# A fused attention and routed feed-forward kernel: x's second half rounded two beats later, and the first batch's ranks counted one tile a slot

## The reference, cut to what matters

```python
x = layernorm(x + attention(x))     # x: 8 x 1024 x 512, 16 heads of 32, causal, fp32
x = layernorm(x + ffn(x))
# ffn, for each of the 8 batches of 1024 tokens:
scores = einsum('bsd,d->bs', x, w_router)
top_scores, top_idx = top_k(scores, 512)
h = gelu(x[top_idx] @ W1 + b1)      # 512 -> 2048
x[top_idx] += sigmoid(top_scores)[:, None] * (h @ W2 + b2)
```

## Time and profile before

| | |
|---|---|
| median of 3 runs | 2547.9 us (2544.73 to 2549.32) |
| profiled execution | 2547.39 us, span 2545.7 us |
| mean granted clock of PE | 0.986 of full |
| attention, by the stretches of the trace | up to about 1797 us |
| feed-forward | the rest, PE busy throughout |

### The profile page before, as it was taken

How to read it: one execution, slowest core, us unless ns; L and a number is a source line. 1 busy time by engine, 2 the same in 40 slices (tenths; PEclk the granted TensorE clock), 3 DMA queues, 4 the chain that set the end, 5 groups by cost and what they waited for, 6 DMA issues and landing times.

```text
span 2545.7 us, 40833 instructions
## 1 busy us (share of the span) xinstructions
PE 2463.0 (97%) x14168; PEld 1824.9 (72%) x14168; DVE 1663.5 (65%) x4230; ACT 1190.7 (47%) x2035; POOL 1565.3 (61%) x1642
## 2 busy tenths in 40 slices
PE   8999999999999999999999999997999999999998
PEld 6666676766777677667767767763688888888886
DVE  7767677677776777767777777676555544553533
ACT  3665566566566556556656566555431111111110
POOL 2878778788887788778788877786232113121311
PEclk9999999999999999999999999998999999999999
DMA  4233435335344433434434344343420001010000
GB/s 174 89 126 127 146 138 191 126 125 177 127 149 159 144 134 135 171 128 169 141 127 159 129 165 149 136 159 96 158 84 28 31 26 42 25 34 25 24 27 17
DMA packets 167502, 287.45 MB, mean 113 GB/s; under 512 B 23241, under 2 KB 58121, under 8 KB 166026
## 3 DMA queue, kind: packets, MB, share of 16 engines
q1 hardware_dynamic: 160130, 267.99, 30.0%
q0 software_dynamic: 7168, 16.85, 2.1%
HBM read 116.97 MB, written 65.11 MB: 72 GB/s over the span
## 4 chain that ended last, share of the span: by engine, by line
PE 73%; POOL 7%; ACT 4%; issue 3%; DVE 2%; DMA 1%; SPq 0%; POOLq 0%; DVEq 0%; ACTq 0%
PE PS L1525 14%; PE PS L1504 13%; PE PS L1363 8%; PE PS L1451 8%; PE PS L1417 7%; PE PS L1469 7%; PE PS L1377 6%; PE PS L1371 6%; POOL Pa L830 5%; DMA h_s<-hs 1%; PE PS L1386 1%; ACT Pm L958 1%; POOL lnrs L843 1%; ACT hs L1011 1%; ACT xb L1013 1%
## 5 line engine op out<-in xcount | busy, mean ns | idle before, releaser
L830 POOL TENSOR_TENSOR Pa<-Pa,Pm 128x512 f32<-128x512 f32 (+1 forms) x602 | 740.7, 1255 | 108.2 <-ACT Pm L958 94.8
L1451 PE MATMUL PS<-Qp,Kp 128*128 128x512 f32 (+3 forms) x1536 | 490.9, 356 | 35.6 <-ACT Pm L958 20.1
L1417 PE MATMUL PS<-Kp,Qp 128*128 128x512 f32 (+3 forms) x1536 | 490.1, 354 | 13.7 <-DVE nm L1055 7.5
L958 ACT ACTIVATE Pm<-PS 128x512 f32<-128x512 f32 (+1 forms) x643 | 358.2, 568 | 278.6 <-PE PS L1451 240.1
L1055 DVE TENSOR_REDUCE nm<-PS 128x1 f32<-128x512 f32 x512 | 345.7, 688 | 181.8 <-PE PS L1417 181.4
L830 POOL TENSOR_TENSOR Pa<-Pa,P 128x512 f32<-128x512 f32 (+1 forms) x297 | 368.2, 1264 | 55.7 <-ACT P L958 49.2
L1451 PEld LDWEIGHTS PS<-Qp,Kp 128*128 128x128 f32 x1536 | 279.6, 191 | 115.4 <-ACT Pm L958 33.8
L1417 PEld LDWEIGHTS PS<-Kp,Qp 128*128 128x128 f32 x1536 | 281.0, 192 | 112.9 <-issue 43.5
L920 ACT ACTIVATE G<-PS,b1c 128x512 f32<-128x512 f32 x128 | 88.1, 688 | 539.7 <-PE PS L1504 539.7
L1063 DVE CUSTOM_DVE_ANT_0 PS<-PS,maskA 128x384 f32<-128x384 f32 (+3 forms) x512 | 245.7, 509 | 140.4 <-PE PS L1417 139.4
L1063 DVE CUSTOM_DVE_ANT_0 PS<-PS,maskA,nm 128x384 f32<-128x384 f32 (+3 forms) x512 | 266.3, 555 | 88.4 <-PE PS L1417 83.4
(11 more groups left out here) (143 smaller groups left out, 4237.4 us busy)
## 6 DMA issues: line engine op xcount, KB each, us to landing
Qp<-nat SPq DMA_DIRECT2D x192, 256.0 KB, 2.5
Kp<-nat SPq DMA_DIRECT2D x192, 256.0 KB, 2.9
o_s<-Of SPq DMA_DIRECT2D x64, 256.0 KB, 2.1
Ot<-o_s SPq DMA_DIRECT2D x64, 256.0 KB, 3.0
xb<-in_x SPq DMA_DIRECT2D x64, 256.0 KB, 3.0
h_s<-hs SPq DMA_DIRECT2D x64, 256.0 KB, 2.4
out<-xb SPq DMA_DIRECT2D x64, 256.0 KB, 2.5
x_raw<-in_xt SPq DMA_DIRECT2D x15, 1024.0 KB, 6.0
```

The lines of the kernel that those rows point to most:

```text
L830: e.tensor_tensor(to, to, probs(u, k)[:, h0:h0 + many, 0:w], ALU.add).then_inc(s["padd"], many)
L958: e.activation(probs(u, k)[:, hh[0]:hh[-1] + 1, 0:w], tile_bank(j)[:, 0:len(hh) * w].rearrange("p (h n) -> p h n", n=w), ACT.Exp).then_inc ...
L1417: ins = e.matmul(to, Qp[:, u % 4, h_, qt * P:qt * P + P], Kp[:, (2 * i + k0 // 512) % 4, h_, 0:w], start=True, stop=True)
L1451: ins = e.matmul(tile_bank(j)[:, x_ * w:x_ * w + w], Kp[:, (2 * i + k // 4) % 4, h_, k % 4 * P:k % 4 * P + P], Qp[:, u % 4, h_, 512 - w:51 ...
```

## The change

1. ACT makes the high parts of the second half of x (batches 1 to 7) at the 7th and 8th beat after its load, instead of the 5th and 6th; DVE its four low parts at beats 8 to 11 after the load, instead of 6 to 9 (so at 128b - 13 to 128b - 10). For the first half DVE's four low parts are spread over beats 6, 8, 10 and 12 after the load instead of 6 to 9.
2. Batch 0's ranks: count t stands 11 beats after output tile 32 + t (beats 697, 713, ..., 809, one a slot, in slots 43 to 50), the list at beat 825, POOL's eight scatters at beats 830, 842, ..., 914, the load of the list at 1024, the gather at 1026. The scratch of the comparison is the hs buffer of output tile 32 + t, already stored and scored by then; ACT waits for the count before it writes that buffer again.
3. The copy of the scores (`srow0`) gets 4 KB of its own, taken from `nat`, which keeps two buffers instead of three.
4. From beat 992 POOL's part of the LayerNorm stands ahead of the additions of its beat.
5. `w1_hi` is at beats 1022, 1024, 1026, 1028, 1038, 1040, 1042, 1044, and `w1_lo` two beats later.

```diff
+GATHER = 63 * 16 + 18
+NORM_FIRST = 62 * 16
...
-            srow0 = ff.enter_context(nc.sbuf_tensor("srow0", [P, N], F32))
-            cmpb0 = ff.enter_context(nc.sbuf_tensor("cmpb0", [P, N], BF16))
...
-        nat = sb("nat", [P, 3, 2, 512], F32R)
+        nat = sb("nat", [P, 2, 2, 512], F32R)
+        srow0 = sb("srow0", [P, N], F32)
...
-            return s["nat", T.nat[job] % 3], 48 * (T.nat[job] // 3 + 1)
+            return s["nat", T.nat[job] % 2], 48 * (T.nat[job] // 2 + 1)
...
+        x_hi, x_lo = {}, {}
+        for n, (b, c) in load_x.items():
+            first = 7 if b and c else 5
+            for half in range(2):
+                x_hi[n + first + half] = b, c, half
+            for k in range(KT):
+                x_lo[n + first + 1 + (2 * k if b and not c else k)] = b, c, k
...
-        rank_at = BEATS * (U - 1) - 2
-        rank_beat = {rank_at + 2 * t: t for t in range(TT + 1)}
-        list_beat = {rank_at + 2 * TT + 1 + t: t for t in range(TT)}
-        list_load, gather_beat = rank_at + 3 * TT + 2, rank_at + 3 * TT + 4
+        RANK_O = 8 * (B - 4)
+        rank_beat = {T.beat[T.o_jobs[RANK_O + t]] + 11: t for t in range(TT + 1)}
+        rank_at = min(rank_beat)
+        list_beat = {max(rank_beat) + 5 + 12 * t: t for t in range(TT)}
+        list_load, gather_beat = GATHER - 2, GATHER
...
-        w1_hi = {BEATS * (U - 1) + 14 + 2 * k: divmod(k, 2) for k in range(8)}
-        w1_lo = {BEATS * (U - 1) + 16 + 2 * k: divmod(k, 2) for k in range(8)}
+        w1_at = [BEATS * (U - 1) + x_ for x_ in (14, 16, 18, 20, 30, 32, 34, 36)]
+        w1_hi = {n: divmod(k, 2) for k, n in enumerate(w1_at)}
+        w1_lo = {n + 2: divmod(k, 2) for k, n in enumerate(w1_at)}
...
             for n in range(T.first, T.last):
+                norms = [o_number(j) for j in o_beat.get(n - 1, ())]
+                if n >= NORM_FIRST:
+                    for o in norms:
+                        layer_norm(o)
                 for u, k in T.steps_formed(n):
...
-                for j in o_beat.get(n - 1, ()):
-                    o = o_number(j)
...
+                if n < NORM_FIRST:
+                    for o in norms:
+                        layer_norm(o)
...
-                        if j >= 3:
-                            e.wait_ge(s["nat", j % 3], 48 * (j // 3))
-                        e.activation(nat[:, j % 3, 0, :], bank(job), ACT.Identity, bias=bA[:, col:col + 1]).then_inc(s["kq_hi"], 1)
+                        if j >= 2:
+                            e.wait_ge(s["nat", j % 2], 48 * (j // 2))
+                        e.activation(nat[:, j % 2, 0, :], bank(job), ACT.Identity, bias=bA[:, col:col + 1]).then_inc(s["kq_hi"], 1)
...
+                    if RANK_O + 2 <= o < RANK_O + TT + 2:
+                        e.wait_ge(s["v_rank"], 2 * (o - RANK_O - 1))
                     e.activation(hs[:, k, :], xb[:, k, :], ACT.Identity, bias=lnb[:, k, 0:1],
...
-                if n - 5 in load_x:
-                    split_x(*load_x[n - 5], 0)
-                if n - 6 in load_x:
-                    split_x(*load_x[n - 6], 1)
+                if n in x_hi:
+                    split_x(*x_hi[n])
...
-                        count_ranks(e, s, cs, sc[:, 0, :], srow0, cmpb0, t)
+                        e.wait_ge(s["score"], RANK_O + t + 1)
+                        count_ranks(e, s, cs, sc[:, 0, :], srow0, hs[:, (RANK_O + t) % 2, :].bitcast(BF16), t)
...
-                for k in range(KT):
-                    if n - 6 - k in load_x:
-                        split_x(*load_x[n - 6 - k], k)
+                if n in x_lo:
+                    split_x(*x_lo[n])
```

More of the change, by code:

```diff
@@ L691, in sync @@
                         dst = Kp[:, (2 * i + c) % 4, :, :]
-                    j = T.nat[job] % 3
+                    j = T.nat[job] % 2
                     for r, part in ((1, 0), (2, 1), (3, 0)) if job[0] == "Q" else ((1, 0), (2, 0), (3, 1)):
@@ L727, in sync @@
                 if n == rank_at - 2:
-                    for j in range(3):
-                        e.wait_ge(s["nat", j], 48 * (len(T.nat) // 3))
                     e.wait_ge(s["scd"], 16)
@@ L741, in sync @@
                 if n == list_load:
+                    for j in range(2):
+                        e.wait_ge(s["nat", j], 48 * (len(T.nat) // 2))
                     load_list(0)
@@ L779, in gpsimd @@
             e.memset(ones[:, :].bitcast(F32), 1.0).then_inc(s["ones"], 1)
-            links = 0
+            links = [0]
             def gather(b):
@@ L808, in keep, with layer_norm @@
                                 pattern=[[0, HG], [1, P]], channel_multiplier=-1).then_inc(s["keep"], 1)
+            def layer_norm(o):
+                k = o % 2
+                e.wait_ge(s["lmva"], o + 1)
+                if o >= 2:
+                    e.wait_ge(s["oset"], o - 1)
+                v = lmv[:, k, 1:2]
+                e.tensor_scalar(lrs[:, k, 0:1], v, EPS, 1.0, ALU.add, ALU.mult)
+                e.tensor_scalar(lrs[:, k, 1:2], v, 1.0 + EPS / 4, EPS * EPS / 4, ALU.mult,
+                                ALU.add).then_inc(s["p_link"], 1)
+                e.wait_ge(s["p_link"], links[0] + 1)
+                e.tensor_tensor(lrs[:, k, :], lrs[:, k, :], cs["half"][:], ALU.pow).then_inc(s["p_link"], 1)
+                links[0] += 2
+                e.wait_ge(s["p_link"], links[0])
+                e.tensor_scalar(lnb[:, k, :], lrs[:, k, :], lmv[:, k, 0:1], -1.0, ALU.mult,
+                                ALU.mult).then_inc(s["rs"], 1)
             for n in range(T.first, T.last):
+                norms = [o_number(j) for j in o_beat.get(n - 1, ())]
+                if n >= NORM_FIRST:
+                    for o in norms:
+                        layer_norm(o)
                 for u, k in T.steps_formed(n):
@@ L852, in gpsimd @@
                     e.tensor_scalar(w, w, 1.0, 2.0, ALU.add, ALU.mult).then_inc(s["p_link"], 1)
-                    e.wait_ge(s["p_link"], links + 1)
+                    e.wait_ge(s["p_link"], links[0] + 1)
                     e.tensor_tensor(w, w, cs["minus"][:], ALU.pow).then_inc(s["sig"], 1)
-                    links += 1
+                    links[0] += 1
                 if n in list_beat:
@@ L1098, in evacuate @@
                     e.wait_ge(s["kq_hi"], j + 1)
[L1099 to L1102, removed]
+                    if j >= 2:
+                        e.wait_ge(s["nat", j % 2], 48 * (j // 2))
+                    e.scalar_tensor_tensor(out=nat[:, j % 2, 1, :], in0=src, scalar=bA[:, col:col + 1],
+                                           in1=nat[:, j % 2, 0, :].bitcast(F32), op0=ALU.add,
                                            op1=ALU.subtract).then_inc(s["ev_v"], 1)
@@ L1585 @@
               "ghi", "glo", "dn", "q_clear", "k_ones")
-SLOTTED = {"xraw": 2, "of_st": 2, "nat": 3, "ost": 2, "hst": 2, "xb": 2, "lst": 2, "x0": 4, "rw": 8, "li": 2, "hg": 2, "fo": 4, "no_shift": 4}
+SLOTTED = {"xraw": 2, "of_st": 2, "nat": 2, "ost": 2, "hst": 2, "xb": 2, "lst": 2, "x0": 4, "rw": 8, "li": 2, "hg": 2, "fo": 4, "no_shift": 4}
 def program(nc, x, xt, wqkv, wo, bat, b_out, w_router, W1, b1, W2, b2, out):
```

## The result

The changed kernel takes 2579.15 us by the median of four runs (2568.61 to 2582.38), the kernel before 2546.32 us on the same chip (four runs, 2543.61 to 2549.32). The ratio is 1.0121, 95% interval 1.0102 to 1.014: slower, as forecast, by 31 us instead of 10 (33 by the medians), and 2 us beyond the upper end of the range. The profiled execution is the shortest of the four, 2568.6 us with a span of 2566.9; the other three have a mean granted clock of 0.983 or 0.984 instead of its 0.988.

The account below looks back on a forecast made before the run. PE, busy 97% of the span, was taken as the bound, so only its waits or half-clock time could be won. 2547.4 + 18 - 12.5 + 4 = 2556.9, say 2557 us; range, 8 in 10, 2532 to 2577.

Parts of the forecast that it names:

- part 1: Moving x's high and low parts at seven batch boundaries: +18 us, bounds -3 and +43.
- I take 1.0, nearer the median: Length assumed for each DVE low part before the second Q; median 0.69 us, at most 1.81, 1.64 beside POOL's additions.
- rival A': Each low part beside a POOL addition takes 1.64 us: fourth ready at 16.7, +30 us for x's beats, 2569 us; chance 0.14.
- The clock: PE's clock falls behind the new wait at the second Q: 1.7 us charged per batch, as behind the old 2.88 us wait.
- The exp: PE's 2.88 us wait for an exp where a batch begins: about 1.8 go, 1.0 us stays.
- The two short waits among the next exps: ACT's two x roundings, now among the next exps, cost PE perhaps 0.9 us; second Q reached about 11.9 us after K.
- The first half's spread: Spreading the first half's low parts costs 0.3 us a batch, 2 us in all (bounds 0 and 0.7 each).
- `nat`: Two buffers make the second Q's evacuation wait for K's copies: covered, 0; 0.5 us waits would give 2573, chance 0.05.
- Part 2: Last slots of the attention, freed of ranks, scatters and four W1 roundings: -12.5 us, bounds -4 and -19.
- First stretch: 1712 to 1747 us: rank counts leave DVE, POOL (27.1 of 35 us) then ends last; 6 us won, at most 7.9.
- Second stretch: 1747 to 1798 us: scatters leave POOL, W1 roundings leave ACT's exps; 6.5 us won with the clock, of 0 to 11.3.
- Part 3: Ranks in their new place, eight counts on DVE and eight scatters on POOL: +4 us, bounds 0 and 12.

## Why the prediction was right and wrong

Right in direction and in mechanism: the wait moved from the exp to the second Q at seven boundaries and weighs more than the end wins. Too low by 22 us: 16 of them in part 1 (18, measured 34 with x's beats alone), 6 in parts 2 and 3 (-8.5, measured -2 without x's beats).

**Part 1, the step that failed: "I take 1.0, nearer the median", and with it the score at its best 0.7.** The fourth low part was put at 9.2 + 1.1 + 0.7 + 0.8 + 3.0 = 14.8 us after the K. Measured, in the same order: low part 2 begins at 10.3 (low part 1, which I took as over, waited 1.85 us for ACT's late rounding and ended behind it); then 0.6 for it, 1.1 for the maxima, 1.35 for the score, 1.66 for low part 3, 0.8 for the maxima, 1.54 for low part 4, together 17.35. Term by term the missing 2.55 us are 1.1 of start, 0.8 of low parts (3.8 instead of 3.0) and 0.65 of score. The start is the same 10.3 with the additions cut away, and there each low part takes 0.69 instead of my 1.0, so that the two errors nearly cancel, 14.75 against 14.8; the additions put 2.63 us on top. The median could not say so. In the trace before, 31 of the 56 low parts took 0.68 to 0.74 us, the other 25 took 1.05 to 1.81: the median lies in the short group, and tells nothing of one that begins beside an addition. The row that answered was 1.64 us, with the 1.6 of the score.
That was rival A' (0.14): ready at 16.7, part 1 at +30. The ready time was 17.35, so A' is met and a little exceeded. The rule of the Trainium skill that stood beside it (SBUF — State Buffer, the section on the two separate sides) agrees with the trace: DVE's instructions that read two SBUF tiles, the score among them, took 1.24 to 1.74 us where they began beside POOL's and 0.69 without, those that read PSUM did not change, and low part 2, which began 0.1 us ahead of POOL's masking, kept its 0.68 us while the masking took 1.07.

**The clock.** I charged 1.7 us behind the new wait. It was 1.7 at batch 2, 1.5 at batch 3, 2.9 and 3.0 at batches 4 and 5, nothing at batch 1 in one execution and 3 us there in another kernel's. With 3.1 for the wait that gives 4.6 to 6.1 us at batches 2 to 5, against 2.2 forecast. Over the seven boundaries the six us behind the wait lose 12.5 us in the changed kernel and 16.2 in the kernel with x's beats alone, where I had charged 7 x 1.7 = 11.9: in the profiled execution this term was about right, and the wait was what I had too short.

**The exp.** Of 2.88 us I let 1.0 stay, 1.65 did. The LayerNorm came back to 1.6 us as I had said, but began 0.5 us later because of the first half's spread; without the spread 1.10 stayed, so my 1.0 holds for the second half's beats alone. (Before the change the wait and the clock make 2.88 + 1.7 = 4.6 us, not quite the 4.3 between the two slots.) The two short waits among the next exps came to 0.43 us instead of 0.9, so PE came to the Q 12.6 us after the K, not 11.9.

**The first half's spread and `nat`.** +2 and 0: 2 us measured, but within the intervals; 0 measured. I had priced the spread at 0.3 us a batch; at batch 5 it puts 0.54 us between the K and the second Q, by the late LayerNorm, which stood nowhere in my sum.

**Part 2.** First stretch 6 us by POOL as the next bound: 6.2, and POOL is the fullest there. Second stretch 6.5: 2.9 in the changed kernel. The places of W1's roundings alone are worth 5 us in the times, nearly what I gave the whole, so what failed is the rest. I had written that nothing is won by the earlier gather; it cost a wait of 2.86 us, since POOL's queue is in order and a masking stands behind it. Whether that wait is the missing time isn't shown: with it removed the medians changed by 0.8 us. In the ten traces with the new places of W1's roundings the stretch was 44.5 to 49.7 us long, so one trace does not size it. Which of the gathers, the clock and the rest took it stays open.

**Part 3.** +4: the trace of the run with x's old beats is 5.0 us late ahead of the last slots. In that trace the shift grows by 1.9 us over the eight slots of the counts (43 to 50) and by 5.4 over those of the scatters and the boundary among them. Moving only the scatters took the shifts of slots 53, 54 and 57 away, for 2 to 5 us by the ratios. The larger share seems to lie with POOL's scatters, not with DVE's counts, which no run moved alone.

## To carry to other kernels

When an instruction of DVE that reads two SBUF tiles is moved, look at what POOL does in its new place, and price it by a row from beside such work, not by the median of its line: 0.69 or 1.6 us was most of the loss here. In this kernel the parts that a product waits for were better made early, at the price of a late exp (2.88 us), than late behind DVE's other work (4.82). Spreading has a price too: one low part across POOL's additions lengthened one of them by 0.45 us and made the LayerNorm behind it late. Where an edit bundles several moves, measure them one by one: here one lost 34 us, and the rest, with the high parts together and the scatters moved, came to 10 to 13 under the kernel before.

## What had not been expected of the hardware

The wait at the second Q repeats to 0.05 us at five boundaries (batches 2 to 6), but what the clock does behind it does not: behind 3.44 us PE went on at 2.4 GHz in one execution and at 1.2 GHz for 6 us in another kernel's after 3.48 us, and behind 4.82 us it lost between 1.5 and 3.0 us. The changed kernel's four executions lie 14 us apart, those of the kernel before 6. POOL pays for the overlap too: its masking at 1078.62 took 1.07 us with low part 2 beside it, 0.64 in the same slot of the kernel before with none.
